# A down projection of ten depth tiles as one Strassen product, its sums by accumulating DMAs

## What is computed

```python
gate = x Wg^T + 0.5 (x Ag^T) Bg^T          # 512 -> 1376, adapters chosen per sequence
up   = x Wu^T + 0.5 (x Au^T) Bu^T
act  = silu(gate) * up
c    = act Wd^T + 0.5 (act Ad^T) Bd^T      # 1376 -> 512
nx   = c * rsqrt(mean(c^2) + 1e-5) * ln_w
out  = x + (silu(nx Fg^T) * (nx Fu^T)) Fd^T   # 512 -> 1792 -> 512
```

## Time and profile before

| | |
|---|---|
| Three timed executions | 396.59, 396.95, 397.47 us |
| Median | 396.95 us |
| Profiled execution | span 395.5 us from first to last instruction; its own whole time is not on record, and the median lies 1.45 us above the span |
| PE, DVE, ACT, POOL busy | 391.8, 314.8, 240.8, 10.6 us |
| Down projection on PE | from 124.12 us to 191.67 us of the span |

### The profile page before, as it was taken

How to read it: one execution, slowest core, us unless ns; L and a number is a source line. 1 busy time by engine, 2 the same in 40 slices (tenths; PEclk the granted TensorE clock), 3 DMA queues, 4 the chain that set the end, 5 groups by cost and what they waited for, 6 DMA issues and landing times.

```text
span 395.5 us, 5733 instructions
## 1 busy us (share of the span) xinstructions
PE 391.8 (99%) x1984; PEld 327.3 (83%) x1984; DVE 314.8 (80%) x476; ACT 240.8 (61%) x386; POOL 10.6 (3%) x13
## 2 busy tenths in 40 slices
PE   9999999999999999999999999999999999999997
PEld 5899888888888888888888888888888888888885
DVE  4899979586835869578699787878787869899994
ACT  5969786857574469815745656464646494484740
POOL 6300000000000000000000000000000000000000
PEclk9999999999999999999999999999999999999999
DMA  7640243311111551000400021313130316105112
GB/s 271 182 133 0 83 133 98 110 53 55 53 55 54 164 154 57 2 0 0 159 2 1 12 97 55 106 53 108 60 119 37 89 57 199 55 1 201 54 53 108
DMA packets 14942, 32.42 MB, mean 82 GB/s; under 512 B 2370, under 2 KB 4930, under 8 KB 14914
## 3 DMA queue, kind: packets, MB, share of 16 engines
q1 hardware_dynamic: 13792, 30.22, 23.7%
q10 hardware_dynamic: 1122, 1.84, 1.3%
HBM read 29.95 MB, written 2.10 MB: 81 GB/s over the span
## 4 chain that ended last, share of the span: by engine, by line
PE 99%; DVE 0%; issue 0%; DVEq 0%
PE bank L1365 53%; PE bank L1705 17%; PE bank L1593 14%; PE bank L1511 3%; PE bank L1557 3%; PE bank L1546 3%; PE bank L1375 3%; PE bank L1615 1%; PE bank L1607 1%; PE bank L1505 1%; PE bank L1714 0%; PE bank L1622 0%; DVE act L1354 0%; DVEq L1352 0%
## 5 line engine op out<-in xcount | busy, mean ns | idle before, releaser
L1365 PE MATMUL bank<-xs,ws 128*128 128x512 f32 x840 | 195.0, 390 | 0.0
L1365 PEld LDWEIGHTS bank<-xs,ws 128*128 128x128 f32 x840 | 156.6, 188 | 31.9
L415 ACT ACTIVATE xs<-act 128x512 fp32r<-128x512 f32 x71 | 42.8, 623 | 21.1 <-DVE act L1045 7.6
L1593 PE MATMUL bank<-xs,wdc 128*128 128x512 f32 x240 | 55.7, 390 | 0.0
L1593 PEld LDWEIGHTS bank<-xs,wdc 128*128 128x128 f32 x240 | 44.8, 188 | 9.5 <-issue 0.2
L889 DVE TENSOR_TENSOR xs<-act,xs 128x512 fp32r<-128x512 f32 x71 | 47.5, 685 | 2.7 <-ACT xs L415 2.1
L889 DVE TENSOR_TENSOR ws<-wraw,ws 128x256 fp32r<-128x256 f32 (+2 forms) x45 | 30.0, 668 | 13.0 <-ACT ws L415 12.8
L415 ACT ACTIVATE bank<-bank 128x512 f32<-128x512 f32 x30 | 17.3, 580 | 34.5 <-PE bank L1365 33.7
L415 ACT ACTIVATE mu<-bank 128x512 f32<-128x512 f32 x44 | 26.1, 596 | 20.1 <-PE bank L1365 13.6
L1705 PE MATMUL bank<-xs,vs 128*128 128x512 f32 x168 | 38.2, 389 | 0.0
L1705 PEld LDWEIGHTS bank<-xs,vs 128*128 128x128 f32 x168 | 31.5, 188 | 6.5
(11 more groups left out here) (133 smaller groups left out, 439.5 us busy)
## 6 DMA issues: line engine op xcount, KB each, us to landing
wraw<-wgu_in SPq DMA_DIRECT2D x22, 512.0 KB, 3.3
wdr<-vs_in SPq DMA_DIRECT2D x7, 512.0 KB, 3.6
wraw<-vj_in SPq DMA_DIRECT2D x3, 896.0 KB, 4.7
wdr<-wd_in SPq DMA_DIRECT2D x10, 256.0 KB, 2.7
xa<-xT_in SPq DMA_DIRECT2D x4, 256.0 KB, 4.1
xa<-xT_in ACTq DMA_DIRECT2D x2, 512.0 KB, 4.7
bgu_raw<-bgu_in SPq DMA_DIRECT2D x32, 32.0 KB, 1.9
xres<-xT_in SPq DMA_DIRECT2D x4, 256.0 KB, 3.5
```

Source lines behind the costliest of these rows:

```text
L415: return nc.scalar.activation(out_ap, in_ap, ACT.Copy, scale=scale)
L1365: ins = mm(z[:, :], w_slot(j)[:, w, s, k * P:(k + 1) * P], xs[:, c, r, k, :], start=(start and k == 0 and s == 0 and r == 0), stop=(k == 1 ...
L1593: ins = mm(z[:, :], wd[:, s, h * P:(h + 1) * P], x[r], start=(start and s == 0 and r == 0), stop=False, skip_group_check=True)
```

## The change

The ten depth tiles and the two halves of tokens become one Strassen product: depth halves of five tiles, output halves of two tiles, token halves. Seven products named 11, t2, 21, t3, t4, t1, 22 (in this order on PE), each of five items of two output tiles of three matmuls: 210 matmuls. Tokens' operands t1 to t4 are sums of activations and weights of four products are sums of weight blocks.

- Weight sums: SP loads one block of 128x1280 floats, and POOL issues DMAs that add the others to it in place (`add_w`, 7 of them). The sums of activations are made by DMAs that add SBUF to SBUF (`add_act`, 7), those of the last pair by DVE, and the subtractions for t1 by POOL (3 instructions). The lo parts of the last two products' weights are made by POOL.
- Weights are split in pieces of 1280 columns (`hi_w`, `lo_w`), activations by one or two tiles (`hi_c`, `lo_c`).
- `t_c` is cut into three parts of 48, 16 and 24 matmuls, ahead of group 6, ahead of group 7 and behind product 11. So `place_ad` and the last two chunks of `stack_hi` move to behind group 4 on ACT.
- Weights 10 (of group 8) are split inside group 7 of the first stage.
- Banks are copied between products (`seed`, `keep_u2`, `copy_u3`, `copy_p5`). Output tiles 0 to 3 of half 0 come after t3 and during t4; tiles 2 and 3 of half 1 after t1, tiles 0 and 1 during and after 22, all four made by DVE (`y_1`).
- `sum_squares(0, 0)` stands inside t1; `y_1(0)` and `y_1(1)` stand ahead of `norm(0)` on DVE, `y_1(2)` and `y_1(3)` among the squares of half 1.

```diff
+        CDOWN = (("11", A_BANK), ("t2", B_BANK), ("21", A_BANK), ("t3", B_BANK), ("t4", B_BANK), ("t1", P5_BANK), ("22", P5_BANK))
+        C11, CT2, C21, CT3, CT4, CT1, C22 = range(7)
+        CW_ORDER = (C11, CT2, CT3, C21, CT4, CT1, C22)
...
+        C_PARTS = [((0, 2), (2, 4), (4, 5)) if p % 2 == 0 else ((0, 1), (1, 3), (3, 5)) for p in range(7)]
+        C_PARTS[CT2] = ((0, 1), (1, 3), (3, 4), (4, 5))
...
+            def add_w(n, p, i, j):
+                if n >= 2:
+                    pool.wait_ge(*cw_added(n - 2))
+                nc.gpsimd.dma_start(C_RAW[p], wc_in[i, j].rearrange("p (k m) -> p k m", k=KC), accum_op=ALU.add
+                                    ).then_inc(s_cw_add[n % 2], 16)
+
+            def add_act(n, to, more):
+                if n >= 2:
+                    pool.wait_ge(*t_added(n - 2))
+                nc.gpsimd.dma_start(to, more, accum_op=ALU.add).then_inc(s_t_add[n % 2], 16)
...
+            pool.wait_ge(*cw_loaded(CT2))
+            add_w(S2_21, CT2, 1, 0)
+            pool.wait_ge(*cw_added(S2_21))
+            add_w(S2_22, CT2, 1, 1)
+            pool.wait_ge(s_t, 1)
+            add_act(T3_012, act_c(0, 3, 1), act_c(KC, KC + 3, 1))
...
+            pool.wait_ge(s_clo, 2)
+            pool.wait_ge(*t_added(T3_012))
+            add_act(T2_01, act_c(0, 2, 0), act_c(0, 2, 1))
...
+            add_w(S4_11, C22, 0, 0)
+            lo_w(CT1)
+            for n, (k, end) in enumerate(C_PARTS[CT1]):
+                pool.wait_ge(s_clo, 5 * CT2 + end)
+                for half in range(k // 2, (end - 1) // 2 + 1):
+                    pool.wait_ge(*t_added(T4_01 + half))
+                part = act_c(k, end, 0)
+                nc.gpsimd.tensor_tensor(part, part, act_c(KC + k, KC + end, 1), ALU.subtract).then_inc(s_t1, 1)
+            lo_w(C22)
...
+                for t in range(2):
+                    same, negated = ((slice(0, FC, 2),), slice(1, FC, 2)) if t == 0 else (
+                        (slice(1, FC, 2), slice(FC - 1, FC)), slice(0, FC - 1, 2))
+                    for e in range(2):
+                        raw, to = ad_raw[:, 4 * t + e:4 * t + 4:2, :, :], ad[:, 2 * t:2 * t + 2, :, 2 * RANK * e:2 * RANK * e + RANK]
+                        for tiles in same:
+                            copy(to[:, :, tiles, :], raw[:, :, tiles, :]).then_inc(s_ad, 1)
+                        copy(to[:, :, negated, :], raw[:, :, negated, :], -1.0).then_inc(s_ad, 1)
...
+                if j == S1 - 1:
+                    hi_c(C11, 0)
                 if w_next(j) < last:
                     hi_a(w_of(w_next(j)))
                 if j != S1 + 3:
                     cu(j)
+                if j == S1 - 1:
+                    hi_c(C11, 1)
...
             for j in range(S1):
-                group(j, S1)
+                group(j, S1 + 1)
...
-                elif j < 6:
+                elif j < 4:
                     stack_hi(j // 2 + 2, j % 2)
+                elif j == 4:
+                    stack_hi(4, 0)
+                    stack_hi(4, 1)
+                    place_ad()
+                elif j == 5:
+                    hi_w(C11, cw_loaded(C11))
                 elif j == 6:
-                    place_ad()
...
+            def last_pair_sums():
+                v.wait_ge(s_t, 3)
+                nc.vector.tensor_tensor(act_at(KC - 1, 1), act_at(KC - 1, 1), act_at(2 * KC - 1, 1), ALU.add).then_inc(s_last, 1)
+                v.wait_ge(s_last, 1)
+                nc.vector.tensor_tensor(act_at(KC - 1, 0), act_at(KC - 1, 0), act_at(KC - 1, 1), ALU.add).then_inc(s_last, 1)
...
+            def y_1(i):
+                h = Y_ORDER[1][i]
+                if h >= 2:
+                    v.wait_ge(s_pc, COPY_P5 + h - 1)
+                    v.wait_ge(s_y, h + 3)
+                    ins = nc.vector.scalar_tensor_tensor(nx1[:, h, :], D_BANK[h - 2][:, :], -1.0, nx1[:, h, :], ALU.mult, ALU.subtract)
+                else:
+                    v.wait_ge(s_y, h + 7)
+                    v.wait_ge(s_clo, 7 * KC)
+                    ins = nc.vector.tensor_tensor(nx1[:, h, :], du2[:, h, :], P5_BANK[h][:, :], ALU.add)
+                ins.then_inc(s_ev[1], 1)
 
...
-                    if 1 <= j < 7:
+                    if 1 <= j < 5:
                         stack_lo((j - 1) // 2 + 2, (j - 1) % 2)
+                    elif j == 5:
+                        stack_lo(4, 0)
+                        stack_lo(4, 1)
+                    elif j == 6:
+                        lo_w(C11)
...
                 if j == S1 - 1:
-                    lo_wd(0)
-                    lo_ac(0)
+                    lo_c(C11, 0)
+                    lo_w(CT2)
+                    lo_c(C11, 1)
...
             c22_sum(S1 - 1)
             c22_act(S1 - 1)
-            lo_wd(1)
-            lo_ac(1)
+            lo_c(C11, 2)
+            lo_w(CT3)
+            lo_c(CT2, 0)
             c21(S1 - 1)
...
+            lo_c(CT1, 0)
             add_square(0, 1)
+            lo_c(CT1, 1)
             add_square(0, 2)
-            lo_ac(20)
+            lo_c(CT1, 2)
+            lo_c(C22, 0)
             add_square(0, 3)
             sum_lo(0)
-            lo_ac(21)
+            lo_short(1)
+            lo_c(C22, 1)
+            lo_c(C22, 2)
+            y_1(0)
+            y_1(1)
...
             sums(G1 + 3)
-            lo_a(G1 + 3)
-            lo_b(G1 + 3)
             first_square()
             add_square(1, 1)
+            y_1(2)
+            lo_a(G1 + 3)
             add_square(1, 2)
+            lo_b(G1 + 3)
+            y_1(3)
             sum_lo(1)
             last_square()
...
+                    t_c_of_pairs(2)
+                    t_c(range(6))
+                elif j == S1 - 1:
+                    t_c_of_pairs(3)
+                    t_c(range(6, 8))
...
-            def down(z, wd, x, h, start):
+            def c_tile(u, h):
+                p, k = u // KC, u % KC
                 for s, r in PASSES:
-                    ins = mm(z[:, :], wd[:, s, h * P:(h + 1) * P], x[r],
-                             start=(start and s == 0 and r == 0), stop=False, skip_group_check=True)
+                    ins = mm(CDOWN[p][1][h][:, :], C_W[p][:, s, k, h * P:(h + 1) * P], slot_c(u, r),
+                             start=(p in (C11, CT1) and k == 0 and s == 0 and r == 0), stop=(k == KC - 1 and s == 1),
+                             skip_group_check=True)
...
-            def last_c(t, h):
+            def c_item(u):
+                pe.wait_ge(s_clo, u + 1)
+                c_tile(u, 0)
+                c_tile(u, 1).then_inc(s_cuse, 1)
...
+            def short_c(t, h):
                 for q in range(2):
                     half = slice(256 * q, 256 * q + 256)
                     for s, r in PASSES:
-                        ins = mm(Y_BANK[t][h][:, half], w10[2 * t + q][s][:, h * P:(h + 1) * P], slot_c(11 * t + 10, r)[:, half],
+                        ins = mm(Y_BANK[t][h][:, half], w10[:, 2 * t + q, s, h * P:(h + 1) * P], short_slot(r)[:, half],
                                  start=False, stop=(s == 1), skip_group_check=True)
-                return ins
+                ins.then_inc(s_y, 1)
```

The new order of PE, as written (half 0's group loop has `t_c(range(6))` ahead of group 6 and `t_c(range(6, 8))` ahead of group 7):

```diff
+            for k in range(KC):
+                c_item(k)
+                if k == 0:
                     p4(S1 - 1)
+            t_c_of_pairs(S1 // 2)
+            t_c(range(8, FC))
+            pe.wait_ge(s_pc, SEED + 1)
+            c_tile(KC, 0)
+            pe.wait_ge(s_pc, SEED + 2)
+            c_tile(KC, 1).then_inc(s_cuse, 1)
+            for u in range(KC + 1, 2 * KC):
+                c_item(u)
+            for u in range(KC * C21, KC * C21 + KC):
+                c_item(u)
+            pe.wait_ge(s_pc, KEEP_U2 + 2)
+            for u in range(KC * CT3, KC * CT3 + KC):
+                c_item(u)
+            short_c(0, 0)
+            short_c(0, 1)
+            pe.wait_ge(s_pc, COPY_U3 + 1)
+            for u in range(KC * CT4, KC * CT4 + KC):
+                c_tile(u, 0)
+            short_c(0, 2)
+            pe.wait_ge(s_pc, COPY_U3 + 2)
+            for u in range(KC * CT4, KC * CT4 + KC):
+                c_tile(u, 1).then_inc(s_cuse, 1)
+            short_c(0, 3)
+            for u in range(KC * CT1, KC * CT1 + KC):
+                c_item(u)
+                if u == KC * CT1 + 3:
                     sum_squares(0, 0)
+            short_c(1, 2)
+            short_c(1, 3)
+            pe.wait_ge(s_pc, COPY_P5 + 1)
+            for u in range(KC * C22, KC * C22 + KC):
+                c_tile(u, 0)
+            short_c(1, 0)
+            pe.wait_ge(s_pc, COPY_P5 + 2)
+            for u in range(KC * C22, KC * C22 + KC):
+                c_tile(u, 1).then_inc(s_cuse, 1)
+            short_c(1, 1)
```

574 lines of the change are left out of this document (344 added, 230 removed).

## The result

The changed kernel takes **432.88 us** (median of four runs, 431.75 to 435.26) against 397.21 (four runs): ratio 1.091, 95% interval 1.087 to 1.095. The prediction had the sign and three of the five places where PE waits; its number, 410.7, and its range, up to 418, are missed by far. The profiled execution took 435.26 (the slowest of the four, 2.4 above the median), its span 433.5, so 38.0 us more than the span of before. One execution of a later run, e13 (435.07 us, 1.7% above that kernel's fastest), counts as slow and is left out of its numbers.

What follows compares the result with a forecast made beforehand. PE's stream was taken to bound the kernel. Matmuls -6.8, stalls +2.0, +4.9, +11.3 and clock +2.4 sum to +13.8 us on the span of 395.5: span 409.3, time 410.7, range 404.5 to 418.

Steps and rivals of the forecast that it cites:

- Matmuls: PE's down projection: 210 matmuls of 512 columns instead of 240, at 0.228 us each, -6.8 us.
- Stall A: At p6(5): PE waits for `ca(5)`, behind added `stack` and `ad` copies on ACT, +2.0 us (1.7 to 2.3).
- Stall B: PE waits 4.3 us at product 11 and 0.5 at p4(7) for ACT's and DVE's work, +4.9 together (4.3 to 5.2).
- Stall C: At q1(8) and the squares of half 1: PE waits for DVE's order behind the sixth output, 1.0 and 10.3, +11.3 us.
- lower bound of 9.7: At the squares of half 1: DVE's busy times alone, 20.3 us, against 10.6 of PE.
- The clock: Slower matmuls at the lower clock level after PE idles, behind the ten-us wait at the squares, +2.4 us.
- nothing behind the shorter ones: Behind PE's waits shorter than the ten-us one, slower matmuls were priced at zero.
- At nothing, with the cover named: Accumulating DMAs, POOL's work, bank copies and splits of products t3 to 22 fit beside PE, priced at zero.
- the additions are slow: Rival at products t2, then t3: additions take 10 us each and PE waits, 414 to 418 us, chance 0.1.
- POOL and DVE: Rival: their tensor instructions hold each other up, last products wait 2 to 6 us more, 413 to 417, chance 0.05.

Runs made afterwards that it cites:

- e13: The changed kernel with SP's twelve small loads of the short tile's weights waiting until t2's second activation sum has landed; 432.38 us, ratio 1.083.
- e4: The changed kernel with the norm of half 0 earlier, ahead of half 1's first two outputs on DVE, and ACT's order to match; 428.00 us, ratio 1.079.
- e2: The changed kernel with t2's activation sums made by two DVE additions instead of two accumulating DMAs; 426.45 us, ratio 1.072.
- e1: The changed kernel with the hi part of product 22's weight sums moved behind the squares of half 0 on ACT; 434.16 us, ratio 1.095.
- e8: Not the computation: only transfers, POOL subtractions beside DVE's and matmul bursts, with 1024 bytes of descriptor memory a partition; five 256-row additions started 5.3 us apart.
- e11: The same transfers and bursts as e8, with 4096 bytes of descriptor memory a partition instead of 1024; all five 256-row additions went in 6.2 us.
- e3: The changed kernel with lo parts of weights 10, the second activation pair and t2's weight piece behind group 7's last results on DVE; 433.77 us, ratio 1.090.

## Why the prediction was wrong

By its own steps:

- **Matmuls**, -6.8: right. Product 21, where PE neither waits nor slows, takes 6.96 for 30.
- **Stall A**, +2.0: right, 1.89.
- **Stall B**, +4.9: 4.12, and none at p4(7). The order was read rightly; the last 0.5 was not there, because item 0 itself ran at the low clock (2.69 for 6) and gave DVE the time.
- **Stall C**, +11.3: 1.05, 8.37 and 0.82, together 10.2. The lo part of the squares ended 20.9 us behind the sixth output, for 21.1 forecast. Right in place and size, and e4 shows that order made most of it (10.2 us of waits fall to 3.9). My lower bound of 9.7 was set too low: it left out the 1.0 at q1(8) that the 11.3 contains.
- **The clock**, +2.4: measured 10.8. The step that failed is "nothing behind the shorter ones". The row that I priced it from was right in size (2.4 for one idle PE; 1.5 to 2.5 in the bursts), but I charged one wait of four. Behind 4.1, 8.2 and 4.9 us PE fell to the lower level too, and t4, with a second wait in it, paid 3.8. Behind the 1.9 us of p6(5) it differs from run to run, and why was not found: the same 18 matmuls behind the same wait took 6.0 us in two of nine profiles (the changed kernel, e2) and 4.4 in seven. The Trainium skill ("TensorE: Matmul & The Clock Gate", Part 1) says that an idle array falls back to 1.2 GHz; these rows agree. The granted clock, 1.00 in the earlier trace rows at slow matmuls, did read 0.50 here.
- **"At nothing, with the cover named"**: this step failed by 14.3 us, 8.2 at t2 (e2 takes it away), 4.9 at t4 (e1 does) and 1.1 of the lock in t4. The additions took 4.8 to 11.2 us where 7.8 was allowed. I had compared each transfer's time with its cover by itself; what broke it was the chain: the DMAs of POOL wait for each other (5.1 us ahead of `T2_23`, by the limit on rows that e8 and e11 show; no run lifts it in the kernel), the transfer then takes 3 us more beside SP's small loads (e13), and on ACT one split that waits for it holds the seed copies, as `hi_w(C22)` holds t4's splits. The rival "the additions are slow" had the right place (t2) and 3 to 5 us where 8.2 stood.
- **POOL and DVE**, given 0.05 and 2 to 6 us: the lock exists. In the changed kernel three DVE splits took 6.15 us for some 3.6 and PE lost 1.1 to it; with the order of e1 it would have cost 7.5. The page of the Trainium skill that I named ("SBUF — State Buffer", Summary: rules for kernel authors) says that the second of the two to issue is blocked until the first finishes. 12.67 us agrees and shows more: a DVE instruction waited for five of POOL's in a row.

The terms that I worked out from order and rows were within 1.1 us each; the two that I set to nothing or charged once came out 22.7 us too low (14.3 and 8.4), and the median missed by 22.2. Against the span, where the sum was made, the miss is 24.2: these 22.7, less 2.0 that A to C had too much, and 3.5 outside the terms of the forecast.

## What to carry to other kernels

Where PE is the bound and has no slack, a saving of matmuls is worth its work only if every other engine's list is laid beside the new, shorter one; each wait of the sizes seen here from 2.2 us up is then to be charged with another 1.5 to 2.8 us for the clock (2.8 behind the 5.9 us at t4 in e3, 15 matmuls in 6.32 us for 3.59). A DMA that adds is not a plain load with a longer time: count what is in flight on its queue and what is queued on ACT behind the instruction that waits for it. Don't put elementwise work on POOL beside a DVE that works on two SBUF tensors.

## What was not expected of the hardware

- An accumulating DMA alone: 6.4 us for 640 KB where the plain load took 4.2, and up to 11.2 beside other loads. On POOL's queue fewer than 512 rows were in flight with 1024 bytes of descriptor memory a partition; with four times that, the only other size tried, five additions of 256 rows went out 1.25 us apart instead of 5.3.
- A run of five tensor instructions on POOL held one DVE instruction for 12.67 us (e1).
- A pause of 2.2 us of PE costs as much in slower matmuls (1.5 us) as one of 11.7 (1.7), and one of 3.7 costs more (2.5).
